# Spreading the softmax denominators: a float32r matmul on rows that hold a high and a low part

## The chip, the cores and the metric

The kernel runs on one core of one Trainium2 chip. The metric is the device time of one execution in microseconds (us); a time given for a kernel is the median of its runs.

## The reference

An early-fusion block for a batch of 8. What matters here is the attention and what is around it:

```
h = tokenise(x) @ W.T             # (8, 1024, 64): a short Fourier transform of patches
h = concat([h, txt], axis=1)      # (8, 1056, 64)
q, k, v = split(layernorm(h) @ w_qkv.T)            # 4 heads of 16
attn = softmax(q @ k.T * SCALE)                    # (8, 4, 1056, 1056), float32
h = h + (attn @ v) @ w_proj.T + b_proj
h = h + moe_ffn(layernorm(h))     # 8 experts, top 2 of the gate, float32
```

The softmax's denominator is the sum over keys, one number for each query and head: 4 x 1056 for one batch element.

## The kernel before

Phase 1 tokenises and attends, phase 2 runs the experts. Between the two stands a block boundary: no engine begins phase 2 before all have ended phase 1.

Phase 1 has a prologue, then eight slots, one per batch element (slots 0 to 7), and an epilogue. A slot goes through 99 units on all engines in the same written order. A unit is one bank of scores (128 keys by 384 or 288 queries, L1038) on TensorE and its exponential on ScalarE (L811). Every four units TensorE multiplies the exponentials by the values (L1016) into `o_bank`; the values carry a column of ones, so that row 16 of each 32-row head block collects the denominator. Between the units lie the row maxima of the next batch element (L1075 on TensorE, `max_parts` L887 on VectorE, three banks in rotation) and side steps whose units are listed by hand: loading x, tokenising, projecting, values, and "finish". Slots 1 to 4 are a loop of two iterations with two slots in its body; the others are written out. In slot 7 VectorE also splits the experts' weights into bf16 parts. The order of work is fixed by these lists; there is no planner.

What the change touches is the way of the denominators of batch element t, taken in the slot of t + 1:

1. Unit 0, SyncE ("spread", 0): after the last evacuation of `heads_out` a transfer brings the four denominator rows, 4 x 1056 numbers, into `den` as 128 x 33 (L713).
2. Unit 8, VectorE ("recip"): a reciprocal of `den` in place (L876). It counts up `recip_done`.
3. SyncE ("spread", 1): it waits for `recip_done` and moves `den` back into row 16 of each 32-row block of `recip_rows`, whose other rows are zero (L717). It counts up `recip_moved`. Behind it in SyncE's queue stand the twelve transfers of "stack" (L703, L704) and the "shift" transfers of the maxima (L738).
4. Units 17, 20, 23, 26, 29 and 32 ("finish", steps 0 to 5), three chunks of 352 columns. In the even steps TensorE multiplies `recip_rows` by the selection matrix `den_sel` (L1147), which copies each head's reciprocal to its 32 rows; ScalarE copies the bank to `recip` (L845) and GpSimd multiplies `on = heads_out * recip` (L776). In the odd steps TensorE projects `on` (L1150) and VectorE adds the result to `h_res` (L954). TensorE waits for `recip_moved` once, in step 0.

For the last batch element these steps stand by themselves in the epilogue, and end with a store of `h_res` (L752). All operands of L1147 are float32.

`den_sel` is a 128 x 128 block of the constants in `cst`. At the start VectorE clears tiles and writes ones, each counted in `preset`, for which TensorE waits.

Of the kernel before, what the change touches and what calls it, by code (L numbers as in the profile page):

```python
# [4 lines left out]

F32 = mybir.dt.float32
BF16 = mybir.dt.bfloat16
I32 = mybir.dt.int32
ALU = mybir.AluOpType
ACT = mybir.ActivationFunctionType  # L10
# [2 lines left out]
P = 128  # L13
# [7 lines left out]
L = IMG + TXT  # L21
H, DH = 4, 16
E, HID = 8, 128
PAIRS = B // 2
CH = L // 3
# [84 lines left out]
N_SETUP = 11  # L110
SHIFT_DMAS = TPC
N_FFN = 8
PRESETS = 21


USES = {"tokenise": 10, "project": 3, "values": 2, "finish": 6}
# [2 lines left out]
def build(nc, x, txt, tok_w, w_qkv, w_proj, b_proj, gate_w, gate_b, w1, b1, w2, b2, consts, out):  # L119
    with ExitStack() as ctx:  # L120
# [68 lines left out]
        preset = sem("preset")  # L189
# [52 lines left out]
        def sb1(name, shape, dt=F32):  # L242
            return phase1.enter_context(nc.sbuf_tensor(name, shape, dt))
# [19 lines left out]
        probs_tail = [sb1(f"probs_tail{i}", [P, WQ]) for i in range(NCH)]  # L263
        ot = [sb1(f"heads_out{i}", [P, L]) for i in range(2)]
        den = sb1("den", [P, H * L // P])
        recip_rows = sb1("recip_rows", [P, L])
        recip = sb1("recip", [P, L])
        on = sb1("on", [P, L])

# [407 lines left out]
        with nc.Block() as block:  # L677


            @block.sync  # L680
            def _(sp):
                sp.dma_start(cst[:, :], consts).then_inc(setup_loaded, 16)
                sp.dma_start(tok_in[:, :, :], tok_w.rearrange("d (r c) -> r d c", c=C)).then_inc(setup_loaded, 16)
                for s in range(2):
                    for half in range(2):
                        sp.dma_start(qkv_in[D * s:D * s + D, half, :],
                                     w_qkv[D * s:D * s + D, :].rearrange("(h d) c -> d h c", h=H))\
                          .then_inc(setup_loaded, 16)
                for half in range(2):
                    sp.dma_start(v_in[:, half, :], w_qkv[2 * D:3 * D, :]).then_inc(setup_loaded, 16)  # L690
                sp.dma_start(bias_in[0:E, :], b1).then_inc(setup_loaded, 16)
                sp.dma_start(bias_in[E:E + E // 2, :], b2.rearrange("(k o) n -> k (o n)", o=2))\
                  .then_inc(setup_loaded, 16)
                sp.wait_ge(preset, 1)
                sp.dma_start(proj_in[:, :, 0:DH], w_proj.rearrange("n (h d) -> n h d", h=H)).then_inc(setup_loaded, 16)
                for k in range(X_DMAS):
                    load_x(sp, 0, k)

                def stack_parts(par, products):
                    for n in products:  # L700
                        a, k = PARTS[n]
                        rows = slice(DH * n, DH * n + DH)
                        sp.dma_start(qs[par][rows, :, 0:L], qk_part[a][0:D, :]).then_inc(stacked, 16)  # L703
                        sp.dma_start(ks[par][rows, :, 0:L], qk_part[k][D:P, :]).then_inc(stacked, 16)  # L704

                def attend_unit(b, par, u, g):
                    pass

                def side(stage, i, t, par, pair, g):
                    if (stage, i) == ("spread", 0):  # L710

                        sp.wait_ge(o_free, NCH * (t + 1))
                        sp.dma_start(den[:, :], ot[par][DH:P:32, :]).then_inc(den_moved, 16)  # L713
                    elif stage == "spread":

                        sp.wait_ge(recip_done, t + 1)
                        sp.dma_start(recip_rows[DH:P:32, :], den[:, :]).then_inc(recip_moved, 16)  # L717
                    elif (stage, i) == ("stack", 0):

                        attended, split = UNITS * (t - 1), NCH * (t + 1)  # L720
                        at_least(sp, scores_ready, attended)
                        sp.wait_ge(part1_done, split)
                        sp.wait_ge(part2_done, split)
                        sp.wait_ge(part3_done, split)
                        stack_parts(par, range(3))
                    elif stage == "stack":
                        stack_parts(par, range(3, 6))
                        if isinstance(t, int) and t == 0:
                            sp.wait_ge(side_full, 3)
                            for k in range(X_EARLY):  # L730
                                load_x(sp, 1, k)
                    elif stage == "shift":

                        c = i[0]
                        sp.wait_ge(shift_step, 4 * (NCH * t + c + 1))
                        for j in range(TPC):
                            first = WQ * c + P * j
                            sp.dma_start(qs[par][ROWS:ROWS + 3, :, first:first + P], m_part[QR * j:QR * j + QR, :])\  # L738
                              .then_inc(shifted, 16)
                    elif stage == "load":  # L740
                        if i == 0:
                            sp.wait_ge(side_free, g)
                        load_x(sp, pair, i)
                    elif stage == "ffn":
                        load_ffn(sp)
                    elif stage == "tokenise" and isinstance(pair, int) and pair == 0 and i == 3:
                        freed(sp, 2, g)
                        sp.dma_start(h_res[:, :], h_new[:, :]).then_inc(h_copied, 16)
                    elif stage == "finish" and i == 5 and par == 1:

                        freed(sp, 5, g)
                        sp.dma_start(h2_all[:, bass.ds(pair, 1), :].rearrange("p o l -> p (o l)"), h_res[:, :])\  # L752
                          .then_inc(h_stored, 16)
                        if not (isinstance(t, int) and t == B - 1):
                            sp.wait_ge(h_stored, 16 * (pair + 1))
                            sp.dma_start(h_res[:, :], h_new[:, :]).then_inc(h_copied, 16)

                run_phase1(nc.sync, attend_unit, side, lambda b, par: None,
                           lambda eng, name, i, p: store_gates(sp, p) if name == "turn" else None)
                sp.wait_ge(ffn_loaded, 16 * N_FFN)  # L760
# [90 lines left out]
            def _(dve):  # L851
# [5 lines left out]
                    nc.vector.memset(v_tail[i][:, :], 0.0).then_inc(preset, 1)  # L857
                    nc.vector.memset(ks[i][ROWS:ROWS + 3, :, :], 1.0).then_inc(preset, 1)
                nc.vector.memset(negm[:, :, :, :, :], 0.0).then_inc(preset, 1)
                nc.vector.memset(recip_rows[:, :], 0.0).then_inc(preset, 1)  # L860
                dve.wait_ge(preset, 11)
                for i in range(2):

                    nc.vector.memset(v_tiles[i][:, :, :, DH:DH + 1], 1.0).then_inc(preset, 1)
                    for h in range(H):
                        nc.vector.memset(v_tail[i][32 * h:32 * h + 32, 32 * h + DH:32 * h + DH + 1], 1.0)\
                          .then_inc(preset, 1)

                dve.wait_ge(setup_psum, 2)
                nc.vector.tensor_copy(tok_m[:, :, :].rearrange("p k d -> p d k"),  # L870
                                      banks[1][:, :].rearrange("p (d k) -> p d k", k=8)).then_inc(setup_done, 1)

                def side(stage, i, t, par, pair, g):
                    if stage == "recip":
                        dve.wait_ge(den_moved, 16 * (t + 1))
                        nc.vector.reciprocal(den[:, :], den[:, :]).then_inc(recip_done, 1)  # L876
                    elif stage == "maxima":
                        c, i, n = i
                        at, place, _ = max_slot(t, c, i, n)
# [108 lines left out]
            def _(pe):  # L988
# [68 lines left out]
                def side(stage, i, t, par, pair, g):  # L1057
# [72 lines left out]
                    elif stage == "tokenise":  # L1130
                        if i < 2:
                            last = embed(bank, i, 7)
                        elif i == 2:
                            last = nc.tensor.matmul(bank[:, 0:TXT], text_in[:, :, :].rearrange("t b d -> t (b d)"),
                                                    ident[0:TXT, 0:TXT], start=True, stop=True)
                        elif i < 6:
                            last = nc.tensor.matmul(bank[:, 0:CH], centre, h_new[:, chunk[i - 3]], start=True, stop=True)
                        elif i == 6:
                            last = token_variances(bank, sq)
                        else:  # L1140
                            last = spread_roots(bank, roots, i - 7)
                    elif stage == "finish":
                        c = i // 2
                        if i == 0:
                            pe.wait_ge(recip_moved, 16 * (t + 1))
                        if i % 2 == 0:
                            last = nc.tensor.matmul(bank[:, 0:CH], den_sel, recip_rows[:, chunk[c]], start=True, stop=True)  # L1147
                        else:
                            pe.wait_ge(on_ready, NCH * t + c + 1)
                            last = nc.tensor.matmul(bank[rows, 0:CH], projT[:, :], on[:, chunk[c]], start=True, stop=True)  # L1150
# [206 lines left out]
def constants():  # L1357
# [7 lines left out]
    c[:, C_CENTRE:C_CENTRE + P] = np.eye(P) - same  # L1365
    c[:, C_MEAN:C_MEAN + P] = same
    c[:, C_TAIL:C_TAIL + TXT] = i[:, None] % 32 == np.arange(TXT)[None, :]
    c[:, C_DEN:C_DEN + P] = (i[:, None] // 32 == i[None, :] // 32) & (i[:, None] % 32 == DH)
    c[:, C_FOLD:C_FOLD + D] = i[:, None] % D == np.arange(D)[None, :]

    t = np.arange(PATCH).reshape(2, 2, 4).transpose(1, 0, 2).reshape(PATCH)
# [25 lines left out]
```

## Time and profile before

| | |
|---|---|
| Median of 3 runs | 1002.04 us |
| The three runs | 1002.44, 1002.04, 996.79 us |
| Profiled execution, its own time | 1001.97 us |
| Span of its instructions | 1000.2 us |
| Mean granted TensorE clock | 0.922 of 2.4 GHz |
| Busy in the span: TensorE (PE), VectorE (DVE), ScalarE (ACT), GpSimd (POOL) | 90%, 57%, 49%, 14% |

The span is from the first to the last instruction of the core; 1.8 us of the execution lie outside. Times in the rows below are from the span's start. PE is a matmul in flight, PEld a load of weights, SPq a transfer issued by SyncE. A float32 matmul call appears as two instructions.

### The profile page before, as it was taken

What the parts mean: (1) busy time and instruction counts of PE and PEld (TensorE: products, weight loads), DVE (VectorE), ACT (ScalarE), POOL (GpSimd) and SP (SyncE); (2) the same over time, 40 slices, a digit from 0 to 9 for tenths busy, and PEclk for the clock granted to TensorE, in tenths of its full rate; (3) what the DMA queues carried; (4) which work ended last, traced back from release to release, by engine and by line L of the source; (5) the groups of instructions that cost most, each with busy time, mean ns of one, the idle gap of its engine ahead of it and who ended that gap; (6) DMA issues with size and microseconds to landing.
All of it is one profiled execution on the core that took longest, in us unless ns stands there. A gap on an engine that the chain in (4) does not pass through costs nothing. (4 is left out here: it accounts for less than half of the span.)

```text
span 1000.2 us, 17890 instructions
## 1 busy us (share of the span) xinstructions
PE 899.0 (90%) x5900; PEld 374.9 (37%) x5900; DVE 573.0 (57%) x1201; ACT 494.4 (49%) x1189; POOL 138.7 (14%) x148
## 2 busy tenths in 40 slices
PE   5665899999999989999999999999965989899996
PEld 5241322433342343343243334333412535354443
DVE  4025565578874557876557887788230553636331
ACT  0020254466664536665446676666533454555552
POOL 0010100011010011101001101001000344444443
PEclk9965589899999988999989999999876999999998
DMA  8329351027551005536002305100006655382731
GB/s 153 57 47 163 62 62 31 3 35 119 97 69 44 2 4 67 117 67 110 2 1 30 40 2 68 44 3 1 1 5 141 120 126 117 80 184 52 155 78 22
DMA packets 55864, 64.58 MB, mean 65 GB/s; under 512 B 23893, under 2 KB 41825, under 8 KB 55777
## 3 DMA queue, kind: packets, MB, share of 16 engines
q1 hardware_dynamic: 55777, 63.46, 35.5%
q8 instruction: 49, 0.80, 0.4%
q14 instruction: 38, 0.31, 0.1%
HBM read 36.73 MB, written 2.43 MB: 39 GB/s over the span
## 5 line engine op out<-in xcount | busy, mean ns | idle before, releaser
L887 DVE TENSOR_REDUCE max_parts<-bank 128x1 f32<-128x512 f32 x512 | 329.6, 685 | 137.4 <-PE bank L1075 134.5
L811 ACT ACTIVATE probs<-bank 128x384 f32<-128x384 f32 (+1 forms) x768 | 313.4, 466 | 191.1 <-PE bank L1038 189.6
L1038 PE MATMUL bank<-q_stack,k_stack 99*128 99x384 bf16 (+1 forms) x768 | 229.9, 329 | 4.9 <-ACT probs L811 4.2
L1075 PE MATMUL bank<-k_stack,q_stack 96*128 96x512 bf16 x512 | 208.4, 409 | 17.2 <-DMA k_stack<-part 13.2
L1016 PE MATMUL bank<-probs,v_tiles 128*32 128x384 f32 (+1 forms) x1536 | 160.2, 490 | 5.4 <-ACT heads_out L796 5.0
L1038 PEld LDWEIGHTS bank<-q_stack,k_stack 99*128 99x128 bf16 x768 | 72.2, 99 | 196.1 <-ACT probs L811 146.1
L1285 ACT ACTIVATE hid<-bank,biases 128x352 f32<-128x352 f32 x192 | 96.0, 552 | 84.8 <-PE bank L1329 84.7
L1304 DVE SCALAR_TENSOR_TENSOR prod<-bank,biases,cwb 128x352 f32<-128x352 f32 x96 | 55.8, 582 | 120.1 <-PE bank L1317 103.0
L1329 PE MATMUL bank<-x,w 128*128 128x352 bf16 (+1 forms) x576 | 105.2, 320 | 6.3 <-DMA x<-part 6.3
L1317 PE MATMUL bank<-hid,w_sb 128*64 128x352 f32 x384 | 79.2, 491 | 7.7 <-DVE prod L1304 4.0
L1052 PE MATMUL bank<-x,tok_m 128*64 128x512 f32 x256 | 68.5, 634 | 9.4 <-DMA text_in<-in_txt 8.0
L1075 PEld LDWEIGHTS bank<-k_stack,q_stack 96*128 96x128 bf16 x512 | 51.4, 101 | 64.9 <-DVE max_parts L887 20.5
L1329 PEld LDWEIGHTS bank<-x,w 128*128 128x128 bf16 x576 | 50.0, 99 | 66.9 <-ACT hid L1285 25.3
L776 POOL TENSOR_TENSOR on<-heads_out,recip 128x352 f32<-128x352 f32 x24 | 22.4, 934 | 353.2 <-ACT recip L845 353.2
L770 POOL TENSOR_TENSOR part<-qk_rest,part 128x352 bf16<-128x352 f32 x24 | 20.4, 850 | 359.5 <-DVE part L935 359.5
L1016 PEld LDWEIGHTS bank<-probs,v_tiles 128*32 128x32 f32 x1536 | 31.1, 110 | 67.2 <-ACT probs L811 42.8
L1267 POOL TENSOR_TENSOR acc<-acc,prod 128x352 f32<-128x352 f32 x48 | 48.4, 1009 | 52.9 <-DVE prod L1304 52.8
L804 ACT ACTIVATE probs_tail<-bank 128x384 f32<-128x384 f32 (+1 forms) x24 | 11.1, 463 | 55.3 <-PE bank L1034 55.2
L1267 POOL TENSOR_TENSOR acc<-prod 128x352 f32<-128x352 f32 x24 | 25.1, 1045 | 84.6 <-DVE prod L1304 84.6
L1317 PEld LDWEIGHTS bank<-hid,w_sb 128*64 128x64 f32 x384 | 19.2, 136 | 36.8 <-issue 24.1
L472 PE MATMUL bank<-cst,roots 128*64 128x128 f32 (+1 forms) x288 | 26.1, 326 | 4.6 <-DVE roots L460 4.4
L1052 PEld LDWEIGHTS bank<-x,tok_m 128*64 128x64 f32 x256 | 15.3, 141 | 35.2 <-issue 32.5
(146 smaller groups left out, 704.2 us busy)
## 6 DMA issues: line engine op xcount, KB each, us to landing
cwb<-gates_by_expert SPq DMA_DIRECT2D x16, 1056.0 KB, 12.1
x<-in_x SPq DMA_DIRECT2D x64, 256.0 KB, 6.9
q_stack<-part SPq DMA_DIRECT2D x48, 132.0 KB, 6.1
k_stack<-part SPq DMA_DIRECT2D x48, 132.0 KB, 6.6
x<-part SPq DMA_DIRECT2D x32, 132.0 KB, 2.5
h_res<-h_new SPq DMA_DIRECT2D x4, 528.0 KB, 3.0
h_all<-h_res SPq DMA_DIRECT2D x4, 528.0 KB, 3.1
h<-h_all SPq DMA_DIRECT2D x8, 264.0 KB, 3.2
```

The costliest lines, as they stand in the source:

```text
L472: last = nc.tensor.matmul(bank[D * bp:D * bp + D, tokens.start - WIDE * i:tokens.stop - WIDE * i], roots[0:n, 2 * t + bp:2 * t + bp + 1].b ...
L811: nc.scalar.activation(probs[:, group % 3, h, 0:n], src, ACT.Exp, scale=SCALE).then_inc(exp_done, 1)
L887: nc.vector.tensor_reduce(max_parts[:, c, H * j + h, i % 2:i % 2 + 1], src[:, :], AX.X, ALU.max)\
L1016: last = nc.tensor.matmul(o_bank[32 * h:32 * h + 32, 0:n], v_tiles[par][:, kt, h, :], probs[:, group % 3, h, 0:n], start=(kt == 0), stop=F ...
L1038: last = nc.tensor.matmul(bank[:, 0:n], ks[par][0:ROWS + 3, h, P * kt:P * kt + P], qs[par][0:ROWS + 3, h, QC[qc]], start=True, stop=True)
L1052: last = nc.tensor.matmul(bank[D * bp:D * bp + D, :], tok_m[:, part, :], xt[bp][:, first:first + NPATCH // 2, t4, :], start=(part == 0), s ...
L1075: last = nc.tensor.matmul(bank[:, :], queries(h, j), ks[par][0:ROWS, h, HALF * (i % 2):HALF * (i % 2) + HALF], start=True, stop=True)
L1267: nc.gpsimd.tensor_tensor(dst, prod[:, 0, :] if k == 1 else dst, prod[:, k, :], ALU.add)\
L1285: nc.scalar.activation(hid[:, e % 4, :], banks[e % 4][:, 0:CH], ACT.Gelu, bias=b1_sb[:, e:e + 1]).then_inc(gelu_done, 1)
L1304: nc.vector.scalar_tensor_tensor(out=prod[:, k, :], in0=banks[4 + k % 2][:, 0:CH], scalar=b2_sb[:, k:k + 1], in1=cwb[bp][:, k, chunk[c]], ...
L1317: last = nc.tensor.matmul(banks[4 + k % 2][D * o:D * o + D, 0:CH], w2_sb[:, e, :], hid[:, e % 4, :], start=True, stop=True)
L1329: last = nc.tensor.matmul(banks[e % 4][:, 0:CH], w[:, e, :], xs[:, bass.ds(b, 1), chunk[c]].rearrange("p o l -> p (o l)"), start=(i == 0), ...
```

## The change

- VectorE writes two new float32r tiles of 128 x 33 after the reciprocal: `den_part0`, the reciprocal rounded to float32r, and `den_part1`, what the rounding left. Each operation waits for the one before, and `recip_done` counts three per batch element. Ahead of the reciprocal VectorE also waits for the transfers of the element before.
- SyncE waits for the third of them and issues two transfers, one for each part: into rows 16 and 17 of each 32-row block of `recip_rows`, now float32r. `recip_moved` counts 32.
- The constant has ones in both rows, and VectorE copies it at the start into a float32r tile `den_pick`, after a wait for the setup transfers. `preset` counts one more.
- The matmul takes `den_pick` and `recip_rows` as float32r. The sum of the two rows is the reciprocal.

```diff
@@ tiles
         den = sb1("den", [P, H * L // P])
-        recip_rows = sb1("recip_rows", [P, L])
+        den_part = [sb1(f"den_part{i}", [P, H * L // P], F32R) for i in range(2)]
+        den_pick = sb1("den_pick", [P, P], F32R)
+        recip_rows = sb1("recip_rows", [P, L], F32R)
@@ SyncE, "spread"
-                        sp.wait_ge(recip_done, t + 1)
-                        sp.dma_start(recip_rows[DH:P:32, :], den[:, :]).then_inc(recip_moved, 16)
+                        sp.wait_ge(recip_done, 3 * t + 3)
+                        for part in range(2):
+                            sp.dma_start(recip_rows.bitcast(F32)[DH + part:P:32, :], den_part[part].bitcast(F32)[:, :])\
+                              .then_inc(recip_moved, 16)
@@ VectorE, setup
-                nc.vector.memset(recip_rows[:, :], 0.0).then_inc(preset, 1)
+                nc.vector.memset(recip_rows.bitcast(F32)[:, :], 0.0).then_inc(preset, 1)
...
+                dve.wait_ge(setup_loaded, 16 * N_SETUP)
+                nc.vector.tensor_copy(den_pick[:, :], den_sel).then_inc(preset, 1)
                 dve.wait_ge(setup_psum, 2)
@@ VectorE, "recip"
                         dve.wait_ge(den_moved, 16 * (t + 1))
+                        at_least(dve, recip_moved, 32 * t)
                         nc.vector.reciprocal(den[:, :], den[:, :]).then_inc(recip_done, 1)
+                        dve.wait_ge(recip_done, 3 * t + 1)
+                        nc.vector.tensor_copy(den_part[0][:, :], den[:, :]).then_inc(recip_done, 1)
+                        dve.wait_ge(recip_done, 3 * t + 2)
+                        nc.vector.tensor_tensor(den_part[1][:, :], den[:, :], den_part[0].bitcast(F32)[:, :],
+                                                ALU.subtract).then_inc(recip_done, 1)
@@ TensorE, "finish"
-                            pe.wait_ge(recip_moved, 16 * (t + 1))
+                            pe.wait_ge(recip_moved, 32 * (t + 1))
                         if i % 2 == 0:
-                            last = nc.tensor.matmul(bank[:, 0:CH], den_sel, recip_rows[:, chunk[c]], start=True, stop=True)
+                            last = nc.tensor.matmul(bank[:, 0:CH], den_pick[:, :], recip_rows[:, chunk[c]], start=True, stop=True)
@@ constants
-    c[:, C_DEN:C_DEN + P] = (i[:, None] // 32 == i[None, :] // 32) & (i[:, None] % 32 == DH)
+    c[:, C_DEN:C_DEN + P] = (i[:, None] // 32 == i[None, :] // 32) & (i[:, None] % 32 // 2 == DH // 2)
```

## Rows read from the trace of the kernel before

**Rows 1.** Busy time by stretch: length, PE, PEld, DVE, ACT, POOL, clock, DMA, GB/s.

```profile
205.00:280.00 75.00, 73.37 (x538) 29.19 (x530) 58.85 (x118) 48.59 (x130) 7.07 (x8) 1.00 0.50 84
660.00:738.00 78.00, 72.26 (x504) 28.19 (x504) 49.15 (x118) 47.20 (x121) 2.81 (x3) 0.91 0.01 3
738.00:763.00 25.00, 9.19 (x14) 2.43 (x13) 2.14 (x4) 3.09 (x5) 2.77 (x3) 0.59 0.15 43
```

**Rows 2.** Timeline of PE in slot 1: start, duration, line, operands, count.

```profile
221.12 0.38 PE L1075 MATMUL bank<-k_stack,q_stack 96*128 96x512 bf16 x1
221.34 0.76 PE L1147 MATMUL bank<-recip_rows,cst 128*128 128x352 f32 x2
221.93 0.33 PE L1038 MATMUL bank<-q_stack,k_stack 99*128 99x384 bf16 x1
```

**Rows 3.** The tile recip_rows: instructions, durations in ns, first and last start.

```profile
L1147 PEld LDWEIGHTS bank<-recip_rows,cst x48: 186/190/338, 221.1 to 753.1; 128*128 128x128 f32 x48
L1147 PE MATMUL bank<-recip_rows,cst x48: 457/459/956, 221.3 to 753.6; 128*128 128x352 f32 x48
L717 SPq DMA_DIRECT2D recip_rows<-den x8: 563/576/586, 217.0 to 741.6; - x8
```

**Rows 4.** Timeline of PE in phase 2: bf16 matmuls at either clock level.

```profile
784.27 1.07 PE L1329 MATMUL bank<-x,w 128*128 128x352 bf16 x6
785.27 0.81 PE L1317 MATMUL bank<-hid,w_sb 128*64 128x352 f32 x4
...
763.78 1.94 PE L1329 MATMUL bank<-x,w 128*128 128x352 bf16 x6 [6.29 <-DMA x<-part]
765.51 1.38 PE L613 MATMUL bank<-h_all,cst 128*128 128x352 f32 x2
```

**Rows 5.** Busy time around the calls in slots 1 and 7; a wait in slot 7.

```profile
217.00:233.00 16.00, 16.00 (x112) 6.04 (x109) 13.13 (x27) 10.81 (x27) 2.56 (x3) 1.00 0.81 105
671.00:687.00 16.00, 15.56 (x107) 5.71 (x106) 15.12 (x30) 10.53 (x26) 2.80 (x3) 1.00 0.01 3
...
699.66 0.38 PE L1097 MATMUL bank<-cst,negm 128*36 128x128 f32 x2 [1.40 <-DVE negm L905]
```

**Rows 6.** Short DVE operations: a group of the slots, and a chain's timeline.

```profile
L455 DVE TENSOR_TENSOR root_work<-roots 128x18 f32<-128x18 f32 x12 | 2.1, 177 | 0.4
...
229.26 0.22 DVE L923 CAST m_mid<-m_rest 36x128 bf16<-36x128 f32 x1
229.58 0.34 DVE L925 SCALAR_TENSOR_TENSOR m_part<-m_mid,cst,m_rest 36x128 bf16<-36x128 bf16 x1
```

**Rows 7.** Timeline of SyncE's transfers in slot 1.

```profile
217.01 0.59 SPq L717 DMA_DIRECT2D recip_rows<-den  x1
217.90 0.61 SPq L703 DMA_DIRECT2D q_stack<-part  x1
218.55 0.59 SPq L704 DMA_DIRECT2D k_stack<-part  x1
...
229.96 2.33 SPq L738 DMA_DIRECT2D q_stack<-m_part  x3
```

**Rows 8.** Timeline of all engines in the epilogue.

```profile
741.20 0.36 DVE L876 RECIPROCAL den<-den 128x33 f32<-128x33 f32 x1 [6.32 <-DMA den<-heads_out]
741.59 0.56 SPq L717 DMA_DIRECT2D recip_rows<-den  x1
...
743.88 1.51 PE L1147 MATMUL bank<-recip_rows,cst 128*128 128x352 f32 x2 [5.36 <-DMA recip_rows<-den]
745.42 0.46 ACT L845 ACTIVATE recip<-bank 128x352 f32<-128x352 f32 x1 [6.46 <-PE bank L1147]
...
747.03 1.41 PE L1150 MATMUL bank<-on,projT 128*64 128x352 f32 x2 [1.65 <-POOL on L776]
...
748.37 1.54 PE L1147 MATMUL bank<-recip_rows,cst 128*128 128x352 f32 x2
...
758.15 0.55 SPq L752 DMA_DIRECT2D h_all<-h_res  x1
759.36 1.28 ACT L1285 ACT_TABLE_LOAD   x1 [4.42 <-PEq L677]
```

More of the change, by code:

```diff
@@ L7 @@
 BF16 = mybir.dt.bfloat16
+F32R = mybir.dt.float32r
 I32 = mybir.dt.int32
@@ L112 @@
 N_FFN = 8
-PRESETS = 21
+PRESETS = 22
 USES = {"tokenise": 10, "project": 3, "values": 2, "finish": 6}
```

## The prediction

> **What bounds the kernel now.** I read the busy time by stretch first [rows 1]. In an attention slot of the loop TensorE has a matmul in flight for 73.37 of 75.00 us at the full clock (1.00 is 2.4 GHz); VectorE is busy for 58.85 and ScalarE for 48.59. In slot 7 (660 to 738 us) TensorE is at 72.26 of 78.00, and in the epilogue (738 to 763 us) at 9.19 of 25.00, with a mean granted clock of 0.59. Busy time of a matmul includes the end of the pipeline, so next I looked at starts in TensorE's timeline around a changed matmul [rows 2]: a score matmul starts at 221.12, L1147 at 221.34, the next at 221.93. None of the rows shows a wait. So the place of L1147 in the stream costs 221.93 - 221.34 = 0.59 us, as two instructions. In all 21 places inside the slots this distance is 0.593 or 0.594 us, and there is no wait on either side. There TensorE's stream sets the time. The tile's own view [rows 3] gives the counts: 48 matmul instructions for 24 calls (three for each of eight batches) and eight transfers.
>
> **The matmul in the slots.** What float32r costs isn't in the trace, so I bound it. Low end: one pass, like bf16. The 512-column bf16 matmul takes 221.34 - 221.12 = 0.22 us from start to start [rows 2], so 352 columns take 0.22 x 352/512 = 0.15; six bf16 matmuls of 352 columns take 785.27 - 784.27 = 1.00 us, 0.167 each [rows 4]. High end: as now, 0.59. The middle case is 0.30, one instruction of today's two. I take 0.15: today's cost is 0.59/0.15 = 4 such passes, as many as there are products of a high and a low half of both operands, and the change hands the two parts over in rows of their own, beside ones that have no low part, so that one pass is all that the result needs. The gain is 0.59 - 0.15 = 0.44 us a call. The weights (0.19 us for 128 fp32 columns [rows 3]) load beside the 0.22 us matmul ahead, and would cost only if they could not.
> The Trainium skill (FP8 and Floating Point Precision, TensorE Precision Notes) says that true FP32 makes four passes, the products of two halves of each operand, while the reduced form reads four bytes and truncates. The four passes agree with the trace, 0.59 against 0.15; that the reduced form takes one is not shown by any row here. By that page the sum would be the one I use.
>
> **How much of it stays.** In a loop slot the stretch around the calls has VectorE busy for 13.13 of 16.00 us and ScalarE for 10.81 [rows 5]. Three calls less 1.33 us leave 14.67 us; VectorE would need 13.13 plus the new 0.45 (below), 93%. So TensorE still leads and I pass the gain on whole. Later stalls in the slot don't take it back, since the engine they wait for had itself been idle waiting for TensorE and moves along. That is six slots (1 to 6), 18 calls, 18 x 0.44 = 7.9 us. In slot 7 VectorE also splits the FFN weights: 15.12 of 16.00 us busy [rows 5], and at 699.66 TensorE waits 1.40 us for it [rows 5]. Of 1.3 us I count 0.5, after VectorE's extra 0.45 is taken off (bounds -0.45, if all of the stretch is VectorE's, and 1.3).
>
> **The longer way to the rows.** VectorE gains a copy and a subtraction of 128x33 after each reciprocal, each waiting for the one before. The nearest rows [rows 6]: a fp32 operation of 128x18 takes 0.177 us, and a 36x128 cast holds 0.32 from its start to the next. I take 0.45 for both with their waits (bounds 0.35 and 0.64). By the formula of the Trainium skill (VectorE: DVE Perf Modes, The TRN2 errata), (N+151)/0.96 ns for a fp32 tensor-tensor operation, the subtraction alone would be an estimated 0.19; the 128x18 row agrees, 0.176 by formula and 0.177 measured.
> SyncE issues two transfers for one. Issues follow each other by 218.55 - 217.90 = 0.65 us [rows 7], so the last one lands 0.45 + 0.65 = 1.1 us later (bounds 1.0 and 1.5). Is that covered in a slot? The issue at 217.01 [rows 7] needs the 2.3 us that the epilogue shows from issue (741.59) to the matmul it frees (743.88) [rows 8], so lands near 219.3, and the first call starts at 221.34 [rows 2], its weights 0.2 before. The slack is 1.8 us (nearly the same in the other slots) against 1.1. It holds with 0.7 to spare: zero. Uncovered, each microsecond over would cost one per slot, seven in all. What is queued on SyncE behind it: the stack's twelve transfers, from 217.90 in the same row group, which move by 1.1 and end near 226.8, before the shift at 229.96 that waits for VectorE anyway; their reader is over twenty units away. On VectorE the row maxima are queued behind the two operations. They fall 0.45 us later, and the three banks take that; TensorE has no wait there now. The guard on the earlier transfers is long met. The setup copy of the matrix and its wait sit where VectorE waits for TensorE's setup product: zero; if not, 0.2 us once.
>
> **The epilogue.** This is a bare chain [rows 8]: reciprocal 741.20, transfer 741.59, L1147 743.88, ScalarE 745.42, L1150 747.03, and L1147 again only at 748.37, three times; then the last store's issue (758.15), and the second phase begins at 759.36. So everything here is on the path. The granted clock is at its lower level, 1.2 GHz: from L1147 to ScalarE 1.54 us. Six bf16 matmuls there take 765.51 - 763.78 = 1.73 us, 0.29 each [rows 4], so three passes fewer take off 0.88 a call (two fewer: 0.59). 3 x 0.88 = 2.6, less the 1.1 of the longer way: 1.5 us gained.
>
> **The sum.** 7.9 + 0.5 + 1.5 = 9.9 us, of the profiled execution's 1001.97 (span 1000.2 and 1.8 around it): 992.1 us. That execution equals the median, 1002.04, to 0.1 us, so the forecast for the median is 992.1. One of the three runs was 996.79, 5.2 below; I allow 2.5 us each way for this alone.
>
> **Rivals.** Each takes the place of one step above.
> *Two passes.* The four-byte operand could stream at half speed, as each of today's two instructions does (0.30). Gains: 18 x 0.30 = 5.4, slot 7 about 0.2, epilogue 3 x 0.59 - 1.1 = 0.7; 6.3 us: 995.7. For it: every four-byte matmul instruction of the trace takes two columns' time per column. Against: those are halves of full precision.
> *No saving (the slower side).* If the matrix engine handles float32r as float32, nothing is saved in the slots, and the longer way remains where nothing covers it: 1.1 us in the epilogue and 0.45 in slot 7: 1003.5. It decides as soon as a call costs more than 0.53 us. The same mechanism is the case in which the change doesn't do what it says.
> *The clock.* Slot 7 is granted 0.91 and not 1.00 [rows 1]; the fall comes around normalisation's thin matmuls and short stalls. Faster calls bring TensorE closer to waits on VectorE. A slot granted 0.91 where it had 1.00 loses 78 x 0.09 = 7 us of the array's full speed, and TensorE sets the time. One and a half more such slots give 992.1 + 10.5 = 1002.6, and the third ends beyond 1% slower. The Trainium skill (TensorE: Matmul & The Clock Gate, Loop structure matters more than you think) says that the loop nest decides whether matmuls stay warm; here the freed place is filled by the next matmul at once, which speaks against this rival.
>
> **How the numbers follow.** One pass 0.67, two passes 0.17, no saving 0.09, clock 0.07. About 1% (10 us) is what this kernel's measurement can tell from no change. The one-pass case centres exactly on that bound, so I split it: 0.33 beyond it, 0.34 within; two passes give 0.02 beyond. Faster 0.36, same 0.61, slower 0.03. The range: 989.0 from 992.1 less spread and a whole slot 7, to 1000.0, past the two-pass case with its spread; beyond it lie the no-saving case and most of the clock's.
>
> **What would show it.** L1147 (L1160 after) with 24 instructions rather than 48, 0.15 us from its start to the next at full clock; busy time of the line down from 22 to some 8 us. A reciprocal followed by two short operations, two issues 0.65 us apart. No wait of TensorE on the rows inside slots; its one wait in the epilogue longer by 1.1 us, and the period of the chain there 3.6 us instead of 4.5. I would be wrong if the call's distance were 0.30 or more, if a wait on the rows appeared in each slot, or if slots shrank by less than 1.3 us because VectorE's maxima set their time instead.

## The result, and the profile after

The changed kernel took 1011.04 us (median of 6 runs, 1006.80 to 1024.02), the kernel before 1001.85 (median of 6). The ratio is 1.0097, 95% interval 1.0064 to 1.0130: about 1% slower, where 1% faster had been forecast. The execution of 1024.02 us belongs to a slower state and is left out of the ratio, as are 1361.3 and 2702.53 us of the kernel before in later comparisons. The profiled execution took 1009.26 us, its span 1007.5.

Line numbers are higher now: the selection matmul is L1160, the projection L1163, the scores L1051 and L1047, the shift transfers L743. The call itself does what was hoped. First the timeline of TensorE in slot 1 of the changed kernel, then the tile den_part:

```profile
215.37 0.38 PE L1088 MATMUL bank<-k_stack,q_stack 96*128 96x512 bf16 x1
215.40 0.52 PE L1160 MATMUL bank<-recip_rows,den_pick 128*128 128x352 f32 x1
215.75 0.34 PE L1051 MATMUL bank<-q_stack,k_stack 99*128 99x384 bf16 x1
```

```profile
L721 SPq DMA_DIRECT2D recip_rows<-den_part x16: 534/554/592, 211.7 to 750.1; - x16
L886 DVE CAST den_part<-den x8: 182/183/184, 211.3 to 749.1; 128x33 fp32r<-128x33 f32 x8
L888 DVE TENSOR_TENSOR den_part<-den,den_part x8: 195/196/197, 211.5 to 749.3; 128x33 fp32r<-128x33 f32 x8
```

The recorded start of the call lies just behind that of its neighbour, so I measure over both: 0.386 us from L1088 to the score matmul (0.379 to 0.386 in 20 of the 21 places inside the slots, 0.405 in one), of which L1088 alone takes 0.22 [rows 2]. That leaves 0.166 for the call, one instruction instead of two; it was 0.593. Each call gives back 0.43 us.

The time went elsewhere. Here is the same engine at the end of that chunk, and then all waits of the execution that end at L1047 (sum, number, longest; one of the six, 2.3 us, is in slot 0 and stands in the kernel before too):

```profile
224.21 0.51 PE L1160 MATMUL bank<-recip_rows,den_pick 128*128 128x352 f32 x1
...
226.38 0.81 PE L1163 MATMUL bank<-on,projT 128*64 128x352 f32 x2
230.09 0.35 PE L1047 MATMUL bank<-q_stack,k_stack 99*32 99x384 bf16 x4 [2.90 <-DMA q_stack<-m_part]
```

```profile
PE bank L1047 <- DMA q_stack<-m_part: 11.4, 6, 2.9
```

L1047 is the first score matmul of the second chunk. Its queries carry the shifts, which SyncE brings with L743. In the kernel before, the same matmul (there L1034) followed the projection at once. There the timeline of TensorE reads:

```profile
233.37 0.81 PE L1150 MATMUL bank<-on,projT 128*64 128x352 f32 x2
234.11 0.35 PE L1034 MATMUL bank<-q_stack,k_stack 99*32 99x384 bf16 x4
```

SyncE's transfers in slot 1, the last stack issue of the kernel before (the others are in [rows 7]) and then the changed kernel:

```profile
225.66 0.60 SPq L704 DMA_DIRECT2D k_stack<-part  x1
```

```profile
211.71 1.17 SPq L721 DMA_DIRECT2D recip_rows<-den_part  x2
213.17 0.60 SPq L706 DMA_DIRECT2D q_stack<-part  x1
...
221.00 0.59 SPq L707 DMA_DIRECT2D k_stack<-part  x1
223.37 2.33 SPq L743 DMA_DIRECT2D q_stack<-m_part  x3
```

The shift is issued 223.37 - 221.00 = 2.4 us after the last issue of the stack; before, 229.96 - 225.66 = 4.3 us. From the first issue of the shift to the chunk's start it was 234.11 - 229.96 = 4.15 us without a wait; now it is 230.09 - 223.37 = 6.72. What the transfers stand behind is seen in the DMA share (the column ahead of GB/s). Busy time by stretch, the kernel before and then the changed one:

```profile
219.00:232.00 13.00, 13.00 (x88) 5.15 (x86) 10.35 (x22) 8.32 (x20) 1.87 (x2) 1.00 0.97 125
232.00:234.00 2.00, 2.00 (x14) 0.45 (x11) 1.50 (x3) 1.38 (x4) 0.94 (x1) 1.00 0.14 20
...
233.00:247.00 14.00, 13.60 (x91) 4.48 (x83) 11.18 (x22) 9.26 (x22) 2.80 (x4) 1.00 0.78 151
```

```profile
214.50:227.50 13.00, 12.68 (x90) 4.41 (x90) 10.96 (x24) 8.25 (x21) 2.82 (x3) 1.00 0.96 123
...
230.00:248.00 18.00, 17.91 (x65) 5.10 (x65) 8.70 (x16) 7.80 (x17) 2.56 (x3) 0.54 0.57 97
```

The twelve stack transfers keep all DMA engines busy for some 13 us, although their issue takes only 8. Before, the stream had all but ended at 232, two microseconds before the chunk.

The trace's records of packets and landings show the same directly. The shift's own packets (36 of 256 bytes) began 1.8 us after its first issue in the kernel before (231.74), and 3.9 us after it in the changed one (227.28), when the stack's packets of 2112 bytes ran out (the last ended at 227.96). The last landing of the shift was at 233.93 before, 0.18 us ahead of L1034, and is at 229.96 now, 0.1 us ahead of L1047, which starts as soon as it may. So the slack in slot 1 had been 0.18 us; in slots 2 to 6 of the kernel before it was 1.97, 0.73, 1.74, 0.17 and 0.04. One part of the delay may have another source than the stack: from the end of the shift's last packet to its last landing it took 2.0 us and not 0.9, while the loads of x, issued at 226.00 right behind the shift (before: 232.59), were already moving. No run separates this part.

Behind the wait comes a second price: from 230 to 248 us the granted clock is 0.54, where the kernel before had 1.00 at that place.

### The profile page after: what moved, and what is told of

It reads as the page before. It is cut to its first block and busy times, and to the rows that moved or that the text cites. A ratio compares the mean times of both kernels' runs of the same rounds, so it can differ in the third digit from the quotient of the medians.

```text
span 1007.5 us, 17881 instructions
## 1 busy us (share of the span) xinstructions
PE 891.3 (88%) x5876; PEld 367.5 (36%) x5876; DVE 575.1 (57%) x1218; ACT 491.9 (49%) x1189; POOL 139.0 (14%) x148
## 3 DMA queue, kind: packets, MB, share of 16 engines
HBM read 36.73 MB, written 2.43 MB: 39 GB/s over the span
## 5 line engine op out<-in xcount | busy, mean ns | idle before, releaser
L1051 PE MATMUL bank<-q_stack,k_stack 99*128 99x384 bf16 (+1 forms) x768 | 229.9, 328 | 4.6 <-ACT probs L816 3.9
L1088 PE MATMUL bank<-k_stack,q_stack 96*128 96x512 bf16 x512 | 207.3, 407 | 18.2 <-DMA k_stack<-part 13.2
L1029 PE MATMUL bank<-probs,v_tiles 128*32 128x384 f32 (+1 forms) x1536 | 162.3, 496 | 5.4 <-ACT heads_out L801 5.0
L1051 PEld LDWEIGHTS bank<-q_stack,k_stack 99*128 99x128 bf16 x768 | 71.5, 99 | 198.6 <-ACT probs L816 147.3
L1088 PEld LDWEIGHTS bank<-k_stack,q_stack 96*128 96x128 bf16 x512 | 51.2, 100 | 64.3 <-DVE max_parts L900 22.8
## 6 DMA issues: line engine op xcount, KB each, us to landing
cwb<-gates_by_expert SPq DMA_DIRECT2D x16, 1056.0 KB, 12.3
```

The source lines that it names most:

```text
L1029: last = nc.tensor.matmul(o_bank[32 * h:32 * h + 32, 0:n], v_tiles[par][:, kt, h, :], probs[:, group % 3, h, 0:n], start=(kt == 0), stop=F ...
L1051: last = nc.tensor.matmul(bank[:, 0:n], ks[par][0:ROWS + 3, h, P * kt:P * kt + P], qs[par][0:ROWS + 3, h, QC[qc]], start=True, stop=True)
L1088: last = nc.tensor.matmul(bank[:, :], queries(h, j), ks[par][0:ROWS, h, HALF * (i % 2):HALF * (i % 2) + HALF], start=True, stop=True)
```

## The experiments

Theory A: the shift transfers land behind the stack's stream; the change starts this stream later (the longer way to the rows) and TensorE arrives earlier (the faster calls), so that a slack of the kernel before turns into a wait, with a fall of the clock behind it. Rival B: the float32r matmul itself lowers the clock. Other rivals stand with the runs.

### The longer way alone

```diff
-        den_part = [sb1(f"den_part{i}", [P, H * L // P], F32R) for i in range(2)]
-        den_pick = sb1("den_pick", [P, P], F32R)
-        recip_rows = sb1("recip_rows", [P, L], F32R)
+        den_part = [sb1(f"den_part{i}", [P, H * L // P]) for i in range(2)]
+        den_pick = sb1("den_pick", [P, P])
+        recip_rows = sb1("recip_rows", [P, L])
```

> The longer way alone: both parts, their two operations on VectorE and the two transfers stay, but all operands of the selection matmul are float32, so that a call costs 0.59 us again. Theory A (the shift transfers of the second chunk land behind the twelve stack transfers, which wait on SyncE for the reciprocals; the chunk's first scores wait for them): the stack starts some 1.3 us later after the reciprocal than before, TensorE arrives when it used to, so its wait ahead of L1047 is 0.5 to 1.5 us in slots 1, 3, 5 and 6, and the epilogue grows by 1.1: 1004 to 1009 us. Rival B (the float32r matmul itself lowers the granted clock): no float32r here, so only the epilogue's 1.1 is left: 1003.

Measured: 1009.99 us (median of 7), ratio to the kernel before 1.0097 (1.0063 to 1.0132). No float32r is left, and it is as slow as the changed kernel, a little slower than the expected 1004 to 1009. So B falls as the main cause. Its timeline of TensorE and a stretch behind the chunk's start:

```profile
227.92 0.81 PE L1163 MATMUL bank<-on,projT 128*64 128x352 f32 x2
230.15 0.35 PE L1047 MATMUL bank<-q_stack,k_stack 99*32 99x384 bf16 x4 [1.43 <-DMA q_stack<-m_part]
...
231.00:247.00 16.00, 16.00 (x60) 4.64 (x59) 8.46 (x16) 7.13 (x17) 2.56 (x3) 0.57 0.56 101
```

The wait is of the expected size, and the clock falls behind it here too. Slots 5 and 6 wait 0.72 and 0.90 us; slot 3, where a wait was expected too, has none.

### The fast matmul alone

```diff
-                        sp.wait_ge(recip_done, 3 * t + 3)
-                        for part in range(2):
+                        sp.wait_ge(recip_done, t + 1)
+                        for part in range(1):
...
-                        nc.vector.reciprocal(den[:, :], den[:, :]).then_inc(recip_done, 1)
-                        dve.wait_ge(recip_done, 3 * t + 1)
-                        nc.vector.tensor_copy(den_part[0][:, :], den[:, :]).then_inc(recip_done, 1)
...
+                            nc.vector.reciprocal(den_part[0][:, :], den[:, :]).then_inc(recip_done, 1)
...
-                            pe.wait_ge(recip_moved, 32 * (t + 1))
+                            pe.wait_ge(recip_moved, 16 * (t + 1))
```

> The fast matmul alone: the reciprocal is written straight as float32r, the low part is left out (no copy, no subtraction, one transfer into row 16; row 17 stays zero). Theory A: the stack starts as before, but TensorE arrives at the second chunk some 1.2 us earlier and waits there for the shift transfers, so that the odd slots and slot 6 give most of their 1.2 us back; slots 2 and 4 and the epilogue (2.6) keep theirs: 996 to 999 us, with waits of 0.5 to 1.3 us ahead of L1047 and perhaps a fall of the clock behind one of them. Rival B: the clock falls as in the changed kernel, 1007 or more. If the cost lay only in the longer way, 990.

Measured: 997.12 us (median of 12, 989.26 to 1002.72), ratio 0.9964 (0.9933 to 0.9994). The calls are fast and nothing on the way to the rows is longer, yet more than half of what they could save by estimate (7.7 us in slots 1 to 6, 1.3 in slot 7, 2.6 in the epilogue) is lost. In slot 1:

```profile
227.51 0.81 PE L1159 MATMUL bank<-on,projT 128*64 128x352 f32 x2
229.88 0.35 PE L1043 MATMUL bank<-q_stack,k_stack 99*32 99x384 bf16 x4 [1.56 <-DMA q_stack<-m_part]
```

Slots 5 and 6 wait 0.88 and 1.14 us. This profiled execution took 992.88 us, with a mean granted clock of 0.931 and no fall behind the waits. Seven of the twelve took 995.65 to 1002.72 us with a mean clock of 0.918 to 0.923; where the clock fell in them isn't in a trace, so the waits (3.6 us) are shown as a cause of the loss, and the rest of the median's is not.

### The stack in two halves, one ahead of the wait for the reciprocals

```diff
             if u == 0 and "finish" in stages:
-                for i in range(2):
-                    order.append(("spread", i, b - 1, 1 - par, q, g))
+                order.append(("spread", 0, b - 1, 1 - par, q, g))
+                if "following" in stages:
+                    order.append(("stack", 0, b + 1, 1 - par, q + 1, g))
+                order.append(("spread", 1, b - 1, 1 - par, q, g))
...
-                for i in range(2):
+                for i in range(1 if "finish" in stages else 0, 2):
```

> The changed kernel, but SyncE issues the first six stack transfers ahead of the wait for the reciprocals and the last six behind it. Theory A: the stack's stream ends 4 us or more earlier, the shift transfers land before TensorE arrives, no wait ahead of L1047 above the 0.39 us of before, no fall of the clock behind it; the gain that was forecast appears: 990 to 994 us. Rival B: the matmuls are unchanged, so the clock and the time stay as in the changed kernel, 1009 to 1012.

Measured: 992.49 us (median of 7, 990.77 to 996.55), ratio 0.9921 (0.9893 to 0.9948). Only the order of SyncE's issues is changed against the changed kernel, and the forecast gain is there. SyncE and TensorE in slot 1, then the stretch behind:

```profile
209.78 0.64 SPq L708 DMA_DIRECT2D q_stack<-part  x1
...
216.26 1.19 SPq L723 DMA_DIRECT2D recip_rows<-den_part  x2
...
221.80 0.60 SPq L709 DMA_DIRECT2D k_stack<-part  x1
228.31 2.33 SPq L745 DMA_DIRECT2D q_stack<-m_part  x3
...
231.31 0.81 PE L1165 MATMUL bank<-on,projT 128*64 128x352 f32 x2
232.05 0.35 PE L1049 MATMUL bank<-q_stack,k_stack 99*32 99x384 bf16 x4
...
232.00:248.00 16.00, 15.56 (x105) 5.48 (x108) 13.29 (x31) 10.55 (x25) 2.56 (x3) 1.00 0.71 134
```

SyncE had stood idle from the fetch of the denominators to the reciprocals; six of the twelve go there. The last stack issue is now 6.5 us ahead of the shift, there is no wait ahead of the chunk, and the clock stays at 1.00 in this stretch. The first selection matmul waits for its rows in slots 1, 4 and 5, by 0.07 to 0.18 us, since six large transfers now stand ahead of them. The profiled execution, 996.55 us, was the slowest of the seven.

### The same order in the kernel before

The same edit of the order in the kernel before.

> The same order of SyncE's transfers in the kernel before. Theory A: its chunk starts did not wait, so there is nothing to take away: 1000 to 1003 us, no change within 0.3%. If the order were worth something by itself, 995 or less.

Measured: 1003.13 us (median of 12), ratio 1.0010 (0.9980 to 1.0039): no gain. The order is worth something only where the chunk waits. It also has a small price of its own: in the profiled execution the first selection matmul waits for its rows in slots 1, 2, 4 and 5, by 0.14, 0.37, 0.71 and 0.34 us, which it did nowhere before. So the nothing is what is left after that price.

### The changed kernel again

> The changed kernel once more, as the mark for the other runs of this call: 1007 to 1013 us.

Measured: 1011.82 us (median of 4, 1007.09 to 1016.25), ratio 1.0118 (1.0066 to 1.0170). The clock fell here too, for 17.1 us from 235.1 on, around the wait of 2.89 us ahead of L1047 at 235.57:

```profile
235.00:252.00 17.00, 16.43 (x47) 4.62 (x48) 7.22 (x14) 6.33 (x14) 2.55 (x3) 0.50 0.64 107
```

The waits ahead of L1047 in the other slots are within 0.1 us of the first profile, but for slot 3 (0.11 us and not 1.69).

### Matmuls in the shadow of the wait

```diff
+                    bank = score_bank[u % 3]
+                    if (r, qc) == (0, 1) and (par == 1 or isinstance(b, int) and b == 6) and not (isinstance(b, int) and b == B - 1):
+                        at_least(pe, exp_done, UNITS * b + u - 2)
+                        for k in range(FILLERS):
+                            nc.tensor.matmul(bank[:, 0:n], ks[par][0:ROWS + 3, k % H, 0:P], qs[par][0:ROWS + 3, k % H, QC[0]],
+                                             start=True, stop=True)
                     if r == 0:
                         pe.wait_ge(shifted, 16 * SHIFT_DMAS * (NCH * b + qc + 1))
                     at_least(pe, exp_done, UNITS * b + u - 2)
-                    bank = score_bank[u % 3]
```

> The changed kernel with twelve bf16 matmuls of 384 columns (some 2 us) in slots 1, 3, 5 and 6, ahead of TensorE's wait for the shift transfers of the second chunk. Their results are overwritten by the chunk's first scores. They lie in the shadow of the wait. Theory A with the clock as its second price (the wait makes the granted clock fall for 17.1, 3.4 and 3.4 us behind it): the chunks start at the same time, the clock doesn't fall behind them, and 12 us of half clock fall away: 999 to 1004 us. If the clock falls for another reason: no change, 1009 to 1012, or up to 2 us more.

Measured: 1003.18 us (median of 12, 998.74 to 1008.69), ratio 1.0039 (1.0011 to 1.0067), 8.6 us below the changed kernel measured beside it. 48 matmuls more make it faster. Slot 1, timeline and stretch:

```profile
229.09 0.81 PE L1169 MATMUL bank<-on,projT 128*64 128x352 f32 x2
229.83 2.12 PE L1045 MATMUL bank<-q_stack,k_stack 99*128 99x384 bf16 x12
232.70 0.35 PE L1053 MATMUL bank<-q_stack,k_stack 99*32 99x384 bf16 x4 [0.74 <-DMA q_stack<-m_part]
...
232.00:248.00 16.00, 14.86 (x99) 5.27 (x100) 12.23 (x28) 9.90 (x24) 2.55 (x3) 1.00 0.70 117
```

L1053 starts at 232.70, 6.61 us after the first issue of the shift, about as late as in the changed kernel (6.72). Summed over slots 1 to 6, the distance from the work ahead (without the added matmuls) to the chunk is 12.3 us, against 12.2 in the changed kernel, and none of the falls behind this wait is left. So the delay stays and the clock's share of the loss is taken off: 8.6 us, about half of the 18.6 that lie between the changed kernel and the one with the stack split.

### Four transfers instead of two

```diff
-                        for part in range(2):
-                            sp.dma_start(recip_rows.bitcast(F32)[DH + part:P:32, :], den_part[part].bitcast(F32)[:, :])\
+                        for part in range(4):
+                            sp.dma_start(recip_rows.bitcast(F32)[DH + part:P:32, :], den_part[part % 2].bitcast(F32)[:, :])\
```

The counts of `recip_moved` go from 32 to 64. The third and fourth transfers go to rows 18 and 19 of a block, which the selection leaves out.

> The changed kernel, but each part is sent twice to the same rows, so that SyncE issues four transfers ahead of the stack, not two. Theory A: the stack starts 1.3 us later, and so the waits ahead of L1047 grow by 1.3 in slots 1, 3, 5 and 6 and by up to 1.3 in 2 and 4, and the epilogue by 1.3; no wait on the rows inside the slots, their slack being larger: 1014 to 1021 us. Rival: if the wait ahead of L1047 has another source (VectorE's maxima), only the epilogue's 1.3 comes on top: 1011 to 1013.

Measured: 1033.88 us (median of 1017.16, 1027.61, 1040.15 and 1044.43), ratio 1.0348 (1.0273 to 1.0422) over all four. They scatter too widely for the size to be trusted; the two lower ones alone give 1022.4. The direction is A's: even the lowest is above the highest of the changed kernel's beside it, 1016.25. Its profiled execution was the fastest, 1017.16: there the distance from the instruction ahead to L1047 (0.39 without a wait in slots 1, 3, 5 and 6, 0.52 in 2 and 4) grew from 3.36, 2.15, 2.44 and 2.60 us in the changed kernel to 4.28, 3.06, 3.41 and 3.52 in slots 1, 3, 5 and 6, by 0.9 to 1.0 each where 1.3 was expected, and in slots 2 and 4 from 0.69 and 0.96 to 2.65 and 2.43. This is 7.2 us more in all, and fits 1017; what the slower three did more isn't in a trace.

### The whole stack ahead of the reciprocals

As in the split, with both halves between the two "spread" steps.

> The changed kernel with all twelve stack transfers issued ahead of the wait for the reciprocals. Theory A in its narrow form (small transfers land behind the bytes that were issued before them): no wait ahead of L1047 any more, but the rows of the reciprocals now land behind the stack's stream of some 13 us, and the first selection matmul of slots 1 to 6 waits 2 to 5 us: 1005 to 1025 us. If small transfers pass the queued ones, 990 to 993, as with the split stack.

Measured: 1035.07 us (median of 4), ratio 1.0361 (1.0312 to 1.0409), slower than the expected 1005 to 1025. SyncE and TensorE in slot 1:

```profile
206.72 0.64 SPq L709 DMA_DIRECT2D q_stack<-part  x1
...
214.90 1.18 SPq L724 DMA_DIRECT2D recip_rows<-den_part  x2
...
216.87 0.38 PE L1091 MATMUL bank<-k_stack,q_stack 96*128 96x512 bf16 x1
223.61 0.66 PE L1163 MATMUL bank<-recip_rows,den_pick 128*128 128x352 f32 x1 [6.37 <-DMA recip_rows<-den_part]
```

No wait ahead of the chunk any more (0.39 in slots 1, 3, 5 and 6), and instead one of 6.37 us on the rows. Slots 2, 4, 5 and 6 wait 6.1 to 6.5 us too, more than the 2 to 5 expected; slot 3 doesn't, and why is open. The two small transfers need 8.7 us from their issue to the matmul that they free, where the epilogue shows 752.35 - 749.52 = 2.8. In these runs a small transfer landed behind the bytes that were issued before it, whichever of the two it was. The Trainium skill (DMA: Bandwidth & Descriptors, Two DMAs through the same engine are not ordered) says that within one queue of one engine descriptors start in order. The runs agree (8.7 us against 2.8); what they show is the landing.

## Why the prediction was wrong

**The step that failed** is the cover of the longer way: "the stack's twelve transfers, from 217.90 in the same row group, which move by 1.1 and end near 226.8, before the shift at 229.96 that waits for VectorE anyway". I compared issues. The stack's issues end at 226, its bytes at about 232, and the shift lands behind them. The issue of the shift does wait for VectorE, as I said, but its landing depended on the start of the stack, which SyncE held back for the reciprocals. The kernel before had no wait above 0.1 us there, and little slack (0.18, 0.17 and 0.04 us in slots 1, 5 and 6): the fast calls alone, some 1.2 us earlier at the chunk, and the longer way alone, which puts the stack's first issue 2.29 us behind the start of the reciprocal (213.17 - 210.88) instead of 1.28 (217.90 - 216.62), each produced a wait (1.56 and 1.43 us in slot 1), both together one of 2.90.

**"So TensorE still leads and I pass the gain on whole"** failed for the same reason. It weighed VectorE's and ScalarE's load, and didn't ask for the DMA engines, with a share of 0.81 in the very row [rows 5], 0.97 from 219 to 232.

**The clock.** I had this as a rival for another reason, closeness to VectorE's waits, and gave it 0.07. It is about half of the loss, but behind waits for transfers, and so my mechanism for it isn't what came; that the rival named the clock is luck. From the start of slot 1 to the end of slot 7 the clock's records show 1.2 GHz for 58.0 us, against 37.5 before. At half speed these 20.5 us cost an estimated 10.2.

**The sum, made again** for the two profiled executions, from the first scores of slot 1 to the last matmul of slot 7: 528.3 us before, 541.5 after, 13.2 longer. Calls: 21 x 0.43 = 9.0 less. The distances ahead of L1047, summed over slots 1 to 6: 9.4 more (12.2 against 2.8). The clock: 10.2 more. That gives 10.6, which leaves 2.6. In slot 7 TensorE stood idle for 1.4 us more (7.1 against 5.7); 1.2 stay open. Ahead of slot 1 the changed kernel was 5.7 us faster (203.74 against 209.49 at its start), in a stretch that the change hardly touches and where the time at 1.2 GHz was 17 us shorter, so the profiled difference of 7.3 us is smaller than the slots' loss.

**What held.** A call: 0.15 forecast, 0.166 measured, one pass; the rivals of two passes and of no saving are out. VectorE's two operations: 0.45 forecast; 0.22 from start to start for the copy and 0.196 for the subtraction. The rows' own slack: no wait on them in any slot. The epilogue:

```profile
749.08 0.18 DVE L886 CAST den_part<-den 128x33 fp32r<-128x33 f32 x1
...
749.52 1.15 SPq L721 DMA_DIRECT2D recip_rows<-den_part  x2
...
752.35 0.63 PE L1160 MATMUL bank<-recip_rows,den_pick 128*128 128x352 f32 x1 [6.34 <-DMA recip_rows<-den_part]
753.01 0.46 ACT L850 ACTIVATE recip<-bank 128x352 f32<-128x352 f32 x1 [6.56 <-PE bank L1160]
```

From TensorE to ScalarE 0.66 us instead of 1.54 [rows 8], the period 755.96 - 752.35 = 3.61, as said; from the last matmul of slot 7 to the second phase 19.9 us instead of 21.6, a gain of 1.7 where 1.5 was forecast.

**Slot 7** was a second, smaller error. It gave nothing of its 0.5 us: 75.3 us long against 73.5, of which 1.7 is more time at 1.2 GHz. But the clock isn't all. With the stack split the slot took 75.5 us with no more time at 1.2 GHz than before (13.7 us), and TensorE was idle in it for 8.7 us and not 5.7; its waits for VectorE's row maxima were 2.1 us and not 1.0. The longer way alone gives 75.4 us, the fast matmul alone 74.6. So the term had the wrong sign and lay beyond its bound of -0.45; which operation of VectorE is behind it, no run isolates.

With the stack split the whole came to 992.49, where 992.1 had been forecast. The missing wait was the large error, but that the two agree so closely is partly luck. In its profiled execution slots 1 to 6 were 8.3 us shorter (7.9 forecast) and the epilogue 1.7 (1.5), but slot 7 was 2.0 longer (0.5 shorter forecast): 8.0 us in all, not 9.9. In the chances, 0.33 and 0.02 make 0.35 for faster, not 0.36.

## What to carry to other kernels

A transfer's issue says little of its landing: look at the DMA share of the stretch, and at how long the queued bytes still run, before calling a small transfer behind a large one covered. When an engine that sets the time gets faster, list all that it waits for just barely not, and look for the slack of each; here a gain of 1.3 us per slot met a slack of less than 0.2 in three of the slots. A wait placed in a queue ahead of work that doesn't need it costs once that work lies on a path: move the free work ahead of it, but only as much as keeps the small transfer's own way open.

## What the runs showed of the hardware

- A float32r matmul of 128 rows and 352 columns took 0.166 us of TensorE's stream, against 0.593 for float32, with one instruction for two. Its load of 128 columns of weights stayed as long (0.19 us).
- Twelve transfers of 132 KB into 16 rows each occupied the DMA engines for some 13 us (share 0.96 and 0.97) and held up small ones issued behind them; 6.4 us of wait in one case.
- A wait of TensorE of 2.90 us, with full work on both sides, was followed by a stretch at 1.2 GHz of 17.1 us; in the run with the longer way alone a wait of 1.43 us was followed by one of 13.7. Behind a wait of 1.56 us, with the fast matmul alone, the profiled execution had none, nor was there one behind 2.14 us in slot 6 of the changed kernel; behind 3.82 us, with four transfers, it was 6.8 us. The kernel before has such a place too: 2.75 us idle ahead of slot 3, then 10.2 us at 1.2 GHz from 373.8 on. So the length of the wait alone doesn't say how long the stretch is; what else does stays open. Twelve matmuls whose results nobody reads, put in the wait, took the fall away and 8.6 us off the time.
